# Four-layer cross-attention on one core: engine orders and PSUM seats made anew from the fifth group's first layer on

## The chip, the core and the metric

The kernel runs on one core of a Trainium2 chip. Its time is device microseconds (us) of one execution. The kernel before was run three times: 557.09, 555.94 and 558.67 us, median 557.09.

## What is computed

The input is x (64 sequences of 128 tokens, 256 features), a context of 64 x 128 x 128 and a second context ("side") of the same shape. Four layers of cross-attention follow each other, all in float32:

```
L0: x = x + softmax(Q K^T / 16) V Wo + bo         Q from x, K and V from ctx
L1: two attentions on normalised x (a: keys from normalised ctx, v: from normalised side);
    x = x + out_a + out_v;  x = x + norm(x) @ fc_W + fc_b
L2: x = norm(softmax over the queries(Q K^T / 16) V + x) * gamma + beta
L3: x = x + softmax(Q K^T / 16) V Wo + bo
```

## The kernel before

**Tiling.** Two sequences make a group; there are 32 groups, each of which passes through all layers. The weights of an attention are folded first (M = Wq Wk^T, N = Wv Wo), so that a layer costs per group: queries (Q), scores (S), a transposition of the probabilities (PT), the weighted context (O) and the projection (OUT). Operands of Q, OUT and a few other products are split into a high and a low part ("hi", "lo"), three products of 256 columns for one. Of the names used below, OUT_fc is the dense part of L1; B2 and V_L2 are the keys' and values' products of L2, made from ctx alone; S_L2 and OUT_L2 are L2's scores and output.

**Engines.** TensorE (PE) does the products, and each result stays in one of eight PSUM banks until ScalarE (ACT) or VectorE (DVE) has read it. ACT does exponentials, copies and "hi" parts, DVE does maxima, sums, "lo" parts and residuals, GpSimd (POOL) does normalisations and row additions, and SyncE (SP) issues every DMA. An attention's last steps are a chain over three engines: PE O_L3, ACT oT_hi_L3 (line 994), DVE oT_lo_L3 (line 1219), PE OUT_L3 (lines 817 to 819). PT_L3 (line 784) likewise goes over ACT's pT_L3 to O_L3 (line 806).

**Through DRAM.** The transposed x of L2 takes a way over DRAM: DVE turns blocks (turn_x3), SP stores them (send_x3, line 638), waits, and loads them back in four DMAs (fetch_x3, lines 640 to 643, issued at line 628). S_L2(g) (line 916, matmuls at line 927) waits for them. The keys of L1 go the same way (send_keys, fetch_keys). Other loads on the same SP queue are load_x (512 KB, line 610), load_ctx (line 614) and load_side (128 KB, line 618); DVE's stats_keys (line 1353) waits for load_side. The store of a group's output is at line 647.

**What sets the order.** Three tables written out by hand or by a planner: STARTS (line 26) has for each of 98 repeated steps 32 numbers, one for a group; PREPARATIONS (line 226) the same for the weights' steps; SEATS (line 243) has the PSUM bank of each use. `timetable()` (line 339) sorts all steps by their number, and each engine's program issues its own steps in that order (`steps_of`, line 545). The numbers have no other use: an engine waits for semaphores alone. COPIES (line 293) has the number of buffers of each tile. A step that takes a bank waits (`bank_for`, line 511) until the bank's last reader has raised its semaphore:

```python
for _, g, name in table:
    if g < 0 and name in preparation:
        preparation[name]()
    elif g >= 0 and name in program:
        program[name](g)
```

Each engine works through its list in order; a step whose input is late holds all that stands behind it on that engine.

Of the kernel before, what the change touches and what calls it, by code (L numbers as in the profile page):

```python
# [50 lines left out]
    "x_bias": [1697, 1869, 2066, 3305, 4131, 5182, 5811, 6496, 10163, 11795, 12108, 12768, 15404, 17497, 18858, 19907, 21118,  # L51
        22461, 24303, 25654, 28257, 29078, 31779, 32290, 33176, 34642, 37610, 38730, 42590, 42715, 43856, 44563],
    "stats_keys": [771, 2568, 3008, 3271, 4384, 4883, 5686, 6916, 7694, 8715, 10618, 13463, 14449, 15514, 16126, 18926, 21377,
        22491, 23556, 24936, 27272, 28423, 29924, 30855, 33415, 35291, 36211, 37748, 39987, 41024, 43612, 44736],
# [1647 lines left out]
```

## Time and profile before

| | |
|---|---|
| median of three runs | 557.09 us |
| span of the profiled execution | 557.1 us (equal to the median run's time) |
| PE, DVE, ACT, POOL busy | 98%, 86%, 80%, 86% of the span |
| matmul records | 4492 |
| DMA | 76.58 MB, 137 GB/s on average |

PE's busy time is the union of its records; a 256-column matmul has a record of 281 ns, and the next one begins about 0.12 us after it, so records overlap. Waits are put down to what ended last.

### The profile page before, as it was taken

Reading aid. Unit: us, or ns where it says so; the run is one execution under the profiler, and the core shown is the slowest. Engines: PE = TensorE matmul, PEld = TensorE weight load, DVE = VectorE, ACT = ScalarE, POOL = GpSimd, SP = SyncE. Lnnn points to the kernel's source line nnn. Section 1 sums busy time; section 2 is a strip of 40 time slices with the busy share of each in tenths; the row PEclk is TensorE's granted clock in tenths of the full one; section 3 lists DMA queues with packets and bytes.
Section 4 is the critical chain, followed back from the end, with each engine's and each line's share of the span. In section 5 each row is a group of like instructions: output and inputs, shape, how many; then the busy total and the mean of one; then the engine's idle time right before and its main releaser. Section 6 shows DMA issues by size and latency. Waiting matters only on the chain.

```text
span 557.1 us, 16210 instructions
## 1 busy us (share of the span) xinstructions
PE 545.8 (98%) x4492; PEld 534.9 (96%) x4492; DVE 478.4 (86%) x1472; ACT 447.2 (80%) x1568; POOL 480.7 (86%) x672
## 2 busy tenths in 40 slices
PE   8999999999999999999999999999999999999995
PEld 7999999999999999989999999999999999999994
DVE  2588799888999889989897997999898987998884
ACT  2799987889778797869879798877888979798663
POOL 4999997999988989979997899977999998766793
PEclk9999999999999999999999999999999999999999
DMA  8993472344553345453247263453433432221112
GB/s 238 352 326 126 118 215 90 121 147 149 172 168 111 113 143 152 149 174 124 80 139 202 67 190 102 145 172 122 139 122 115 124 105 78 77 96 58 39 40 95
DMA packets 74440, 76.58 MB, mean 137 GB/s; under 512 B 7664, under 2 KB 58224, under 8 KB 74352
## 3 DMA queue, kind: packets, MB, share of 16 engines
q1 hardware_dynamic: 74352, 75.55, 43.0%
q8 instruction: 38, 0.62, 0.5%
q14 instruction: 50, 0.41, 0.3%
HBM read 50.87 MB, written 24.64 MB: 136 GB/s over the span
## 4 chain that ended last, share of the span: by engine, by line
PE 87%; POOL 4%; DMA 3%; issue 2%; DVE 2%; SPq 1%; ACT 1%; DVEq 0%; POOLq 0%; ACTq 0%
PE bank L793 15%; PE bank L806 10%; PE bank L800 9%; PE bank L776 7%; PE bank L817 5%; PE bank L819 5%; PE bank L818 5%; PE bank L949 5%; PE bank L927 5%; PE bank L784 5%; PE bank L830 4%; PE bank L902 3%; PE bank L903 3%; PE bank L904 3%; DMA side_in<-in_side 1%
## 5 line engine op out<-in xcount | busy, mean ns | idle before, releaser
L1065 ACT ACTIVATE prob_L<-bank,neg_max_L 128x128 f32<-128x128 f32 x320 | 114.5, 375 | 15.7 <-DVE neg_max_L L1376 13.6
L1065 ACT ACTIVATION_READ_ACCUMULATOR prob_L<-bank,neg_max_L 128x1 f32 x320 | 68.3, 214 | 0.0
L1376 DVE TENSOR_REDUCE neg_max_L<-bank 128x2 f32<-128x256 f32 (+1 forms) x128 | 60.5, 479 | 7.1 <-PE bank L800 4.3
L1546 POOL TENSOR_TENSOR rstd_ln<-var_eps_ln,minus_half 128x2 f32<-128x2 f32 x64 | 45.2, 707 | 18.5 <-ACT var_eps_ln L1078 18.2
L994 ACT ACTIVATE oT_hi_L<-bank 128x256 fp32r<-128x256 f32 (+1 forms) x96 | 44.4, 471 | 12.4 <-PE bank L806 11.1
L1219 DVE TENSOR_TENSOR oT_lo_L<-bank,oT_hi_L 128x256 fp32r<-128x256 f32 (+1 forms) x96 | 47.2, 501 | 5.6 <-ACT oT_hi_L L994 4.9
L994 ACT ACTIVATE probT_L<-bank 128x256 f32<-128x256 f32 (+1 forms) x96 | 44.4, 470 | 9.0 <-PE bank L784 8.6
L1333 DVE BATCH_NORM_STATS2 stats_ln<-x 128x6 f32<-128x256 f32 x128 | 47.5, 413 | 0.2
L1219 DVE TENSOR_TENSOR xT_lo_L<-bank,xT_hi_L 128x512 fp32r<-128x512 f32 x64 | 43.1, 677 | 3.7 <-ACT xT_hi_L L994 3.5
L1611 POOL TENSOR_TENSOR x_bias<-x,bias_fc 128x512 f32<-128x512 f32 x32 | 41.1, 1285 | 5.8 <-DVE x L1409 5.8
L1588 POOL TENSOR_TENSOR xT_lo_L<-x_in,xT_hi_L 128x512 fp32r<-128x512 f32 x32 | 41.2, 1286 | 5.4 <-ACT xT_hi_L L994 5.4
L1597 POOL TENSOR_TENSOR x_bias<-x_in,bias_L 128x512 f32<-128x512 f32 x32 | 41.1, 1285 | 3.7 <-DVE x L1403 3.7
L994 ACT ACTIVATE xT_hi_L<-bank 128x512 fp32r<-128x512 f32 x64 | 38.7, 610 | 6.8 <-PE bank L776 4.3
L1628 POOL TENSOR_TENSOR x_res<-x_res,bias_L 128x512 f32<-128x512 f32 x32 | 41.1, 1285 | 2.5
L817 PE MATMUL bank<-N_hi_L,oT_hi_L 128*128 128x256 f32 x128 | 40.1, 314 | 2.7 <-DVE oT_lo_L L1219 2.7
L784 PE MATMUL bank<-ident,prob_L 128*128 128x128 f32 x256 | 42.6, 273 | 0.2 <-ACT prob_L L1065 0.2
L1604 POOL TENSOR_TENSOR x_bias<-x,bias_L 128x512 f32<-128x512 f32 x32 | 41.2, 1286 | 1.8 <-DVE x L1403 1.3
L1171 ACT ACTIVATE prob_L<-prob_L,inv_total_L 128x128 f32<-128x128 f32 x128 | 41.5, 418 | 1.3 <-DVE inv_total_L L1383 1.2
L1626 POOL TENSOR_TENSOR x_res<-xhat_ln,gamma_row 128x512 f32<-128x512 f32 x32 | 41.2, 1287 | 1.4 <-DVE y L1403 1.1
L793 PE MATMUL bank<-xT_hi_L,M_hi_L 128*128 128x256 f32 x128 | 40.2, 314 | 0.0
L800 PE MATMUL bank<-ctx_in,qT_L 128*128 128x128 f32 x256 | 38.5, 275 | 0.5 <-ACT qT_L L1127 0.3
L806 PE MATMUL bank<-probT_L,ctx_in 128*128 128x128 f32 x256 | 38.5, 275 | 0.0
(228 smaller groups left out, 2294.2 us busy)
## 6 DMA issues: line engine op xcount, KB each, us to landing
x_in<-in_x SPq DMA_DIRECT2D x32, 512.0 KB, 3.8
ctx_in<-in_ctx SPq DMA_DIRECT2D x32, 256.0 KB, 2.8
keys_out<-keys_turned SPq DMA_DIRECT2D x32, 256.0 KB, 2.2
keysT<-keys_out SPq DMA_DIRECT2D x128, 64.0 KB, 2.0
out<-y SPq DMA_DIRECT2D x32, 256.0 KB, 2.3
x_out<-x_turned SPq DMA_DIRECT2D x30, 256.0 KB, 2.2
x3T<-x_out SPq DMA_DIRECT2D x120, 64.0 KB, 2.3
side_in<-in_side SPq DMA_DIRECT2D x32, 128.0 KB, 2.7
```

The lines of the kernel that those rows point to most:

```text
L784: last = tr(block(bank, b), src[:, b, :], ident[:])
L793: last = mm(bank[:, i * TOK:(i + 1) * TOK], w[:, t, :], x[:, t, :], start=t == 0 and n == 0, stop=t == T - 1 and n == 2)
L800: last = mm(block(bank, b), block(at(qT[k], g), b), kT[:, b], start=True, stop=True)
L806: last = mm(block(bank, b), natural[:, b, :], block(at(probT[k], g), b), start=True, stop=True)
L817: mm(to, h, N_h[:], start=i == 0, stop=False)
L994: activation(to, of, ACT.Copy).then_inc(done[step], 1)
L1065: last = activation(at(prob[k], g)[:, b, :], block(bank, b), ACT.Exp, bias=at(neg_max[k], g)[:, b:b + 1], accum_out=at(total[k], g)[:, b:b ...
L1171: last = activation(p[:, b, :], p[:, b, :], ACT.Copy, scale=at(inv_total["L1"], g)[:, b:b + 1])
L1219: dve.tensor_tensor(to, of, hi.bitcast(F32), ALU.subtract).then_inc(done[step], 1)
L1333: last = dve.bn_stats(st[:, n, :], tile)
L1376: dve.tensor_reduce(at(neg_max[k], g)[:], scores, AX.X, ALU.max, negate=True).then_inc(done[f"max_{k}"], 1)
L1546: pool.tensor_tensor(at(rstd[k], g)[:], at(var_eps[k], g)[:], minus_half[:, 0:n], ALU.pow).then_inc(done[f"rstd_{k}"], 1)
```

## The change

STARTS, PREPARATIONS and SEATS have new numbers. Code, operations, sizes, transfers, the counts of steps and COPIES are the same. What that does to the orders, counted over both tables:

| engine | steps | same from the start | of the groups' steps: in another place | moved by at most |
|---|---|---|---|---|
| PE | 760 | 53 | 276 of 738 | 6 places |
| ACT | 821 | 63 | 430 of 802 | 19 |
| DVE | 856 | 54 | 488 of 830 | 14 |
| POOL | 465 | 49 | 190 of 448 | 4 |
| SP | 269 | 48 | 80 of 252 | 4 |

PE's first 53 steps are everything up to O_L0(3); the first other step is Q_L0(4), which now stands ahead of Q_L1(1). The first changed seat is that of O_L0(2). The places of the order that the prediction speaks of, before and after (for PE all steps from the first to the last named are shown):

```
PE before: OUT_fc:16 V_L2:18 PT_L0:21 OUT_L1:17 OUT_L0:19 O_L0:20 B2:19 T_fc:17 O_L0:21 ... OUT_fc:17 S_L2:16
PE after:  V_L2:18 OUT_fc:16 OUT_L1:17 OUT_L0:19 O_L0:20 PT_L0:21 B2:19 T_fc:17 O_L0:21 ... OUT_fc:17 S_L2:16

PE before: OUT_fc:29 T_L3:26 Q_L3:25 PT_L1:31 OUT_L1:30 O_L1:31 Q_L3:26 S_L2:28 T_fc:30 S_L3:25 S_L3:26 OUT_L1:31 OUT_fc:30 S_L2:29
PE after:  Q_L3:25 OUT_fc:29 T_L3:26 PT_L1:31 OUT_L1:30 O_L1:31 Q_L3:26 T_fc:30 S_L2:28 S_L3:25 S_L3:26 OUT_L1:31 OUT_fc:30 S_L2:29

PE before, its last steps: Q_L3:31 PT_L3:30 S_L3:31 OUT_L3:29 O_L3:30 PT_L3:31 OUT_L3:30 O_L3:31 OUT_L3:31
PE after, its last steps:  Q_L3:31 PT_L3:30 S_L3:31 OUT_L3:29 O_L3:30 PT_L3:31 O_L3:31 OUT_L3:30 OUT_L3:31

SP before: send_x3:1 load_x:10 fetch_keys:5 fetch_x3:1
SP after:  send_x3:1 load_x:10 fetch_keys:5 fetch_x3:1

SP before: send_x3:13 load_x:22 fetch_x3:13 load_side:20
SP after:  send_x3:13 fetch_x3:13 load_x:22 load_side:20

SP before: store:19 send_x3:23 fetch_keys:26 load_ctx:30 fetch_x3:23
SP after:  send_x3:23 store:19 fetch_keys:26 fetch_x3:23 load_ctx:30

SP before and after: send_x3:11 store:8 fetch_x3:11 load_side:18
DVE before: stats_lnf:12 inv_L1:13 lo_L1:14 lo_fc:12 max_L2:10 stats_keys:18 oT_lo_L0:15
DVE after:  stats_lnf:12 lo_L1:14 inv_L1:13 lo_fc:12 max_L2:10 stats_keys:18 oT_lo_L0:15
```

Four pairs of PE steps stand much closer after the change: PT_L0(21) to O_L0(21) has 10 matmul records between them (before 32), O_L0(26) to OUT_L0(26) 34 (56), O_L0(11) to OUT_L0(11) 46 (66), O_L3(6) to OUT_L3(6) 14 (26).

The diff replaces some 240 lines of the three tables by as many; seven of the 98 steps of STARTS and one of SEATS stand here:

```diff
...
-    "load_x": [598, 1078, 1126, 1894, 2374, 2725, 3569, 4395, 5587, 6765, 7583, 10302, 12074, 12282, 12907, 15654, 17636, 18997,
-        20046, 21631, 23999, 24736, 25793, 28591, 29405, 31918, 32429, 33813, 36493, 38744, 40228, 42729],
+    "load_x": [601, 1162, 1206, 2146, 2593, 2857, 3698, 4528, 5720, 6938, 7753, 10486, 12264, 12359, 13159, 15955, 18382, 19948, 20287,
+        22107, 24296, 25097, 26385, 29048, 29848, 32379, 33041, 34327, 37241, 39144, 41092, 43370],
...
-    "OUT_fc": [6138, 7159, 7982, 9037, 10990, 13848, 14797, 15736, 16958, 18486, 21833, 22342, 23604, 25187, 27472, 28252,
-        30515, 32012, 34172, 35842, 36837, 37408, 39262, 41138, 43479, 45273, 46832, 48070, 49970, 50536, 51505, 52290],
+    "OUT_fc": [6281, 7303, 8127, 9183, 11169, 14021, 15057, 15973, 17199, 18745, 22153, 22681, 23944, 25531, 27855, 28655, 31011,
+        32458, 34659, 36331, 37345, 37917, 39792, 41708, 44086, 45883, 47483, 48699, 50622, 51279, 52195, 53000],
...
-    "PT_L3": [9824, 10923, 11976, 13647, 15353, 18200, 19683, 20454, 22204, 23332, 26697, 27843, 28951, 29632, 31811, 33532,
-        34855, 37112, 39106, 40148, 41708, 43026, 44424, 46402, 47678, 51910, 51932, 53255, 53348, 53710, 54068, 54358],
+    "PT_L3": [10072, 11148, 12249, 13954, 15590, 18503, 20051, 20801, 22472, 23762, 27061, 28320, 29376, 30059, 32257, 33999, 35345,
+        37531, 39636, 40815, 42254, 43704, 44821, 47033, 48419, 52601, 52623, 53939, 54050, 54421, 54762, 54993],
...
-    "O_L3": [10120, 11154, 12163, 13803, 15535, 18353, 19882, 20610, 22527, 23488, 26807, 28093, 29088, 29909, 31968, 34357,
-        35019, 37221, 39218, 40659, 41804, 43208, 44590, 47086, 48825, 52245, 52431, 53370, 53504, 53862, 54268, 54510],
+    "O_L3": [10373, 11378, 12364, 14163, 15772, 18611, 20323, 20979, 22867, 23900, 27243, 28432, 29513, 30333, 32413, 34802, 35580,
+        37872, 39748, 40979, 42392, 43816, 45199, 47714, 49608, 52955, 53300, 54072, 54206, 54603, 54941, 55083],
...
-    "OUT_L3": [10347, 11455, 12554, 14132, 16337, 19133, 20227, 20936, 22803, 24091, 27213, 28597, 29267, 30129, 32243, 35064,
-        35322, 37732, 39448, 41279, 42128, 43408, 44839, 48212, 50289, 52476, 52861, 53549, 53907, 54197, 54439, 54682],
+    "OUT_L3": [10596, 11655, 12756, 14492, 16664, 19413, 20529, 21237, 23144, 24478, 27597, 28957, 29692, 30554, 32690, 35510, 35855,
+        38285, 39935, 41850, 42717, 44015, 45404, 48863, 50808, 53142, 53565, 54250, 54532, 54870, 55127, 55316],
...
-    "V_L2": [2417, 2675, 3265, 4136, 5334, 6750, 7735, 9409, 10808, 12092, 16135, 17144, 18972, 19997, 22226, 23217, 25738,
-        27888, 30657, 31354, 32549, 33114, 33855, 37266, 37661, 39035, 40588, 41849, 43850, 44212, 46144, 48327],
+    "V_L2": [2538, 2801, 3383, 4253, 5477, 6893, 7677, 9620, 10989, 12271, 16373, 17385, 19342, 20368, 22565, 23535, 26083, 28184,
+        30940, 31779, 32925, 33652, 34322, 37730, 38170, 39565, 41184, 42553, 44459, 44843, 46754, 49069],
...
-    "fetch_x3": [6982, 7851, 8766, 9749, 11882, 14532, 15410, 16351, 17684, 19399, 22498, 23090, 24216, 25848, 28212, 29213,
-        31726, 32921, 34802, 36541, 37672, 38478, 40036, 41974, 44210, 46265, 47556, 48794, 50583, 51216, None, None],
+    "fetch_x3": [7137, 8009, 8880, 9877, 12029, 14800, 15721, 16607, 18148, 19568, 22803, 23438, 24818, 26195, 28598, 29658, 32152,
+        33282, 35264, 36985, 38286, 38954, 40608, 42468, 44867, 46902, 48202, 49480, 51227, 51899, None, None],
...
-    "N_L1v": [5],
+    "N_L1v": [2],
```

## Rows read from the trace of the kernel before

**Rows 1.** The page's first two parts, whole span: busy us (share) and count; granted clock.
```profile
PE 545.8 (98%) x4492; PEld 534.9 (96%) x4492; DVE 478.4 (86%) x1472; ACT 447.2 (80%) x1568; POOL 480.7 (86%) x672
...
PEclk9999999999999999999999999999999999999999
```

**Rows 2.** The page's fourth part, the chain that ended last, share of span by engine.
```profile
PE 87%; POOL 4%; DMA 3%; issue 2%; DVE 2%; SPq 1%; ACT 1%; DVEq 0%; POOLq 0%; ACTq 0%
```

**Rows 3.** Windows: stretch, length, busy us (count) per engine, clock, DMA share, GB/s.
```profile
0.00:20.00 20.00, 17.45 (x85) 15.46 (x86) 6.64 (x25) 8.08 (x21) 11.73 (x30) 1.00 0.87 271
...
80.00:100.00 20.00, 19.40 (x165) 19.13 (x164) 18.35 (x57) 14.60 (x58) 16.10 (x25) 1.00 0.40 111
...
200.00:250.00 50.00, 48.95 (x416) 48.46 (x415) 44.63 (x138) 40.32 (x140) 43.38 (x61) 1.00 0.49 153
250.00:300.00 50.00, 49.34 (x419) 48.86 (x418) 44.95 (x140) 43.63 (x161) 46.20 (x62) 1.00 0.41 125
300.00:350.00 50.00, 49.72 (x416) 48.86 (x415) 44.02 (x136) 41.95 (x143) 45.74 (x64) 1.00 0.41 129
...
400.00:450.00 50.00, 49.79 (x418) 49.12 (x418) 44.93 (x139) 41.69 (x146) 47.17 (x64) 1.00 0.37 118
...
530.00:557.00 27.00, 21.25 (x160) 18.92 (x158) 17.93 (x50) 13.82 (x50) 17.27 (x24) 0.97 0.21 70
sum 557.00, PE 545.76 PEld 534.93 DVE 478.45 ACT 447.15 POOL 480.67; mean PE 36.38 PEld 35.66 DVE 31.90 ACT 29.81 POOL 32.04
```

**Rows 4.** Windows again, the last stretch alone.
```profile
552.50:557.10 4.60, 0.90 (x6) 0.69 (x6) 0.88 (x2) 0.00 (x0) 0.00 (x0) 0.80 0.34 114
```

**Rows 5.** Chain of waits around S_L2(1) and S_L2(13): start, us, what.
```profile
84.35 0.60 issue
84.94 1.13 PE bank L927 x8
...
266.55 0.66 issue
```

**Rows 6.** Timeline of SP's queue before those two: start, us, issue.
```profile
76.54 0.33 SPq L610 DMA_DIRECT2D x_in<-in_x  x1
...
78.87 1.85 SPq L628 DMA_DIRECT2D x3T<-x_out  x4
...
261.44 0.35 SPq L610 DMA_DIRECT2D x_in<-in_x  x1
261.89 1.80 SPq L628 DMA_DIRECT2D x3T<-x_out  x4
```

**Rows 7.** Chain, then timelines of DVE and PE's loads, before OUT_L0(15).
```profile
234.84 4.52 DMA side_in<-in_side
...
239.46 0.49 DVE L1333 BATCH_NORM_STATS2 stats_keys<-ctx_in 128x6 f32<-128x128 f32 x2 [1.80 <-DMA side_in<-in_side]
...
241.17 0.19 PEld L817 LDWEIGHTS bank<-N_hi_L,oT_hi_L 128*128 128x128 f32 x1 [1.25 <-DVE oT_lo_L L1219]
```

**Rows 8.** Timeline of PE at S_L2(16), then at S_L2(29).
```profile
326.38 0.28 PE L904 MATMUL bank<-F_hi,xT_lo_fc 128*128 128x256 f32 x1
326.57 1.13 PE L927 MATMUL bank<-x3T,B 128*128 128x128 f32 x8
...
522.25 0.28 PE L904 MATMUL bank<-F_hi,xT_lo_fc 128*128 128x256 f32 x1
522.37 1.05 PE L927 MATMUL bank<-x3T,B 128*128 128x128 f32 x8
```

**Rows 9.** Timeline of the last steps: DVE's and ACT's before OUT_L3(30), PE's O_L3(31) and OUT_L3(31).
```profile
549.52 0.41 DVE L1219 TENSOR_TENSOR oT_lo_L<-bank,oT_hi_L 128x256 fp32r<-128x256 f32 x1
549.64 0.38 ACT L994 ACTIVATE probT_L<-bank 128x256 f32<-128x256 f32 x1 [0.25 <-PE bank L784]
...
550.79 0.61 PE L806 MATMUL bank<-probT_L,ctx_in 128*128 128x128 f32 x4
...
552.42 0.39 PE L817 MATMUL bank<-N_hi_L,oT_hi_L 128*128 128x256 f32 x1 [1.02 <-DVE oT_lo_L L1219]
```

More of the change, by code:

```diff
@@ L45 @@
-    "load_side": [214, 1558, 1606, 1654, 4035, 4658, 5462, 6340, 7441, 8164, 10008, 13048, 13987, 14842, 15754, 17902, 20774,
[5 rows of a table removed]
[L51 to L54, printed above, removed]
@@ L211 @@
-    "fetch_keys": [3843, 4466, 4975, 5800, 7201, 7659, 8977, 11642, 13747, 14340, 15211, 16940, 19159, 21191, 22040, 23608,
[11 rows of a table removed]
-}
-PREPARATIONS = {"run_up": 164, "M_L2": 534, "k_L2": 709, "N_L0": 1000, "n_L0": 912, "M_L0": 1364, "M_L1v": 1452, "m_L0": 1541, "m_L1v":
[14 rows of a table removed]
+    "load_x": [601, 1162, 1206, 2146, 2593, 2857, 3698, 4528, 5720, 6938, 7753, 10486, 12264, 12359, 13159, 15955, 18382, 19948, 20287,
[5 rows of a table added]
+    "load_ctx": [257, 1708, 1752, 2285, 2329, 2373, 2417, 2461, 2505, 2549, 10442, 11738, 12433, 14232, 15911, 18680, 20392, 21215,
[3 rows of a table added]
@@ new lines @@
+    "hi_ctx": [813, 2514, 2654, 3319, 3559, 4360, 5652, 7112, 8200, 9728, 11277, 12403, 16506, 17575, 19482, 20823, 23074, 24781,
[5 rows of a table added]
+    "lo_ctx": [863, 2651, 2915, 3685, 5236, 5707, 7118, 7933, 9733, 11799, 12884, 16747, 18431, 20086, 20551, 23231, 24351, 26270,
+        28631, 31280, 31985, 33353, 34121, 34837, 37853, 38572, 40588, 41297, 43363, 44625, 45524, 47495],
+    "load_side": [213, 1796, 1840, 1884, 4094, 4762, 5590, 6497, 7599, 8318, 10170, 13296, 14320, 15442, 16012, 18338, 21098, 22151,
[5 rows of a table added]
@@ new lines @@
+    "x_bias": [1749, 1935, 2128, 3436, 4267, 5306, 5979, 6677, 10335, 11992, 12227, 13027, 15675, 17714, 19097, 20155, 21351, 23107,
+        24682, 26022, 28439, 29484, 32247, 32756, 33668, 35129, 38112, 39111, 43238, 43432, 44376, 45208],
+    "stats_keys": [642, 2698, 3143, 3404, 4534, 5155, 5928, 7079, 7869, 8896, 10819, 13791, 14844, 15781, 16399, 19111, 21725, 23093,
+        23907, 25290, 27649, 29168, 30359, 31290, 33908, 35773, 36749, 38296, 40531, 41597, 44107, 45464],
+    "rstd_keys": [933, 2985, 4087, 4516, 5137, 5812, 6578, 7517, 8376, 10236, 13357, 14531, 15225, 16197, 19289, 23301, 23566, 23665,
[15 rows of a table added]
@@ new lines @@
+    "stats_lnf": [6047, 6984, 7738, 8732, 10614, 13697, 14681, 15480, 16518, 18418, 21630, 22281, 23649, 24836, 27276, 28324, 31033,
+        31877, 34120, 36233, 37000, 37453, 39533, 41308, 43724, 45830, 47097, 48061, 50150, 50587, 51758, 52302],
+    "rstd_lnf": [6510, 7325, 8106, 9369, 10791, 14048, 15157, 15799, 16679, 18643, 21835, 22480, 24082, 25141, 27732, 28843, 31553,
+        32179, 34315, 36419, 37422, 37686, 39968, 41758, 44059, 46293, 47688, 48544, 50416, 51257, 52121, 52448],
+    "lo_fc": [6201, 7207, 7988, 9105, 11058, 13911, 14963, 15900, 16732, 18665, 22035, 22528, 23814, 25231, 27437, 28538, 30854,
+        31971, 34291, 36173, 37257, 37700, 39687, 41471, 43988, 45755, 47375, 48599, 50433, 51048, 51997, 52868],
@@ new lines @@
+    "store": [10799, 12219, 13034, 15486, 17086, 19992, 20730, 21625, 23393, 25052, 28832, 29438, 30346, 30882, 32936, 35739, 36184,
[3 rows of a table added]
+    "eps_keys": [844, 2897, 3589, 3608, 4665, 5773, 6184, 7380, 8338, 9806, 11772, 14445, 14983, 16046, 16620, 20119, 22604, 23406,
[3 rows of a table added]
+    "eps_lnf": [6470, 7239, 8066, 9330, 10720, 13942, 14964, 15688, 16639, 18583, 21736, 22426, 24042, 25077, 27693, 28523, 31139,
[7 rows of a table added]
+    "turn_keys": [1372, 4149, 4929, 5686, 6922, 7419, 8826, 11353, 13529, 14094, 15142, 16095, 18277, 21097, 21904, 23587, 24700, 26772,
+        28664, 30126, 31161, 33748, 35585, 36426, 37194, 38818, 41093, 43826, 45042, 46787, 47668, 49638],
@@ L247 @@
     "n_L0": [2],
-    "B2": [4, 7, 2, 5, 6, 0, 1, 3, 6, 7, 5, 5, 4, 7, 1, 3, 3, 3, 1, 7, 7, 4, 3, 4, 6, 3, 7, 7, 5, 3, 5, 4],
+    "B2": [4, 7, 2, 2, 6, 6, 2, 5, 6, 2, 2, 4, 6, 1, 6, 7, 7, 3, 2, 1, 6, 7, 3, 2, 7, 4, 5, 0, 6, 0, 2, 0],
     "M_L0": [5],
@@ L251 @@
     "m_L0": [7],
-    "Q_L0": [0, 4, 3, 0, 6, 4, 0, 1, 5, 1, 1, 6, 0, 0, 5, 6, 6, 7, 7, 6, 5, 6, 2, 2, 0, 3, 3, 0, 0, 0, 3, 6],
+    "Q_L0": [0, 4, 3, 0, 4, 3, 6, 5, 7, 6, 1, 1, 0, 2, 4, 6, 6, 2, 3, 6, 4, 7, 1, 6, 7, 4, 4, 0, 2, 1, 2, 0],
     "m_L1v": [1],
-    "S_L0": [5, 6, 5, 0, 1, 3, 1, 5, 3, 5, 5, 6, 6, 1, 0, 7, 4, 0, 3, 2, 3, 3, 1, 6, 3, 3, 3, 7, 5, 4, 4, 3],
+    "S_L0": [5, 6, 5, 0, 5, 5, 5, 2, 7, 5, 2, 4, 3, 4, 4, 2, 1, 6, 7, 1, 4, 2, 7, 1, 1, 5, 4, 4, 2, 2, 3, 0],
     "n_fc": [4],
@@ L268 @@
     "M_L1a": [0],
[1 row of a table removed]
[1 row of a table added]
     "mean_M_L1a": [4],
[1 row of a table removed]
[1 row of a table added]
     "m_L1a": [3],
[5 rows of a table removed]
-    "T_fc": [1, 5, 6, 5, 6, 6, 5, 1, 5, 6, 7, 3, 7, 4, 2, 7, 1, 5, 4, 5, 3, 3, 6, 2, 1, 3, 6, 5, 7, 7, 1, 5],
-    "OUT_fc": [1, 5, 6, 5, 5, 5, 0, 1, 5, 6, 1, 7, 7, 6, 4, 0, 2, 2, 0, 6, 2, 4, 3, 2, 1, 3, 6, 7, 3, 7, 3, 0],
[10 rows of a table removed]
[5 rows of a table added]
+    "T_fc": [2, 2, 6, 1, 3, 4, 6, 1, 4, 5, 7, 2, 2, 6, 4, 2, 7, 6, 6, 1, 1, 6, 7, 0, 7, 1, 2, 5, 2, 2, 2, 7],
+    "OUT_fc": [2, 2, 6, 1, 3, 4, 1, 1, 0, 5, 5, 7, 2, 5, 2, 0, 0, 0, 2, 1, 3, 6, 4, 7, 7, 1, 2, 4, 3, 2, 3, 4],
[9 rows of a table added]
 }
```

34 lines of the change are left out of this document (10 added, 24 removed), and 371 rows, old and new, of tables (PREPARATIONS, SEATS, STARTS).

## The prediction

> **What bounds the kernel now.** I read the busy shares first: PE is busy 98% of the span, the next engines 86%, and the granted clock is at its upper level (2.4 GHz) in every slice [rows 1]. The chain that ended last is 87% PE [rows 2]. So the time is PE's work plus the time in which PE stands still, and a change that keeps all operations can only alter the second. I then looked for that in windows [rows 3]: a stretch's length less PE's busy time is its idle time. It is 2.55 us in the first 20 us, 0.60 in 80 to 100, 1.05 in 200 to 250, 0.66 in 250 to 300, 0.28 in 300 to 350, 0.21 in 400 to 450, and 5.75 in the last 27. All together 557.00 - 545.76 = 11.24 us; what those seven leave, 0.14, is scattered. Last I read, for each of the larger ones, what PE waited for, and asked whether the new order changes that wait.
>
> **What can change at all.** The first 2.55 us lie before O_L0(3), where the order is kept. Of the last 5.75 us, 4.60 - 0.90 = 3.70 lie in the stretch that holds only the last projection, the last residual on DVE and the last store [rows 4]; these stay. There remain 2.94 us in the middle (0.60 + 1.05 + 0.66 + 0.28 + 0.21 + 0.14) and 5.75 - 3.70 = 2.05 us near the end, 4.99 us in all. If the new order lost none of it, the time would be 557.1 - 5.0 = 552.1 us. That is the most that can be had by these rows, and more than any single step promises.
>
> The sum is made against the profiled execution, whose span, 557.1 us, is also the median of the three runs (557.09), so nothing is to be added around it.
>
> The Trainium skill (Perfetto Trace Analysis, Identifying the Most-Contended Engine) warns that PE's busy share is no good measure of headroom, as pipelined instructions look smaller in the trace. The rows bear it out in part: records of 0.28 us begin 0.12 us apart [rows 8], so a delay of up to 0.16 us between two matmuls leaves no idle time. By that rule more than 5.0 us could be had; the sum here does without it.
>
> **The end of the kernel.** Before, PE issued OUT_L3(30) ahead of O_L3(31). OUT_L3(30) had to wait for DVE's oT_lo, which ended at 549.52 + 0.41 = 549.93; the copy of probabilities that O_L3(31) needs ended at 549.64 + 0.38 = 550.02 [rows 9]. O_L3(31) nevertheless began only at 550.79, since six projections stood ahead of it. After the change it comes first and can begin at about 550.07 (0.05 after its input). That is 0.72 us earlier. From O_L3(31) to OUT_L3(31) it is 552.42 - 550.79 = 1.63 us, a chain over ACT and DVE; OUT_L3(30) with its six matmuls (6 x 0.12 = 0.7) now fits into it after four records of O_L3(31) (about 0.5). DVE's residual of group 30, which stood ahead of the last oT_lo, comes later, which may give another 0.1. Ends: 0 (if the copy is delayed by as much) and 1.0 (the whole wait at OUT_L3(31)). I take -0.75 us.
>
> **S_L2(13).** PE stood 0.66 us [rows 5] because the four fetches for it, issued from 261.89 on, came right behind a 512 KB load_x issued at 261.44 [rows 6]. The new order puts load_x(22) behind the fetch; PE's steps between OUT_fc(13) and S_L2(13) are the same in number. The fetch is issued 0.45 us sooner and has the DMA engines to itself. Ends: 0.45 (issue alone) and 0.66. I take -0.6 us. S_L2(23) has the same change with a 256 KB load_ctx(30); it holds the 0.21 us of 400 to 450. I take -0.2 us. load_x(22) itself is issued some 2 us later, behind the four fetches (1.80 us [rows 6]); Q_L0(22), the first product that needs it, stands 338 matmul records after S_L2(13) (some 40 us at 0.12), which covers it.
>
> **S_L2(1).** Its 0.60 us [rows 5] have the same cause (load_x issued at 76.54, the fetch at 78.87 [rows 6]), and there the new order is the same. It stays: 0.
>
> **OUT_L0(15).** The largest single wait, 1.25 us seen by PE's loads, came over DVE: stats_keys(18) waited 1.80 us for side_in, which needed 4.52 us to land, and oT_lo_L0(15) stood behind it [rows 7]. SP's order before that load and DVE's order at that place are the same after the change. It stays, unless this load lands faster in that run: ends -1.05 and 0, I take 0. The 0.28 us of 300 to 350 I leave as well.
>
> **New waits.** V_L2(18) now stands ahead of OUT_fc(16), so OUT_fc(16), and all that goes over DRAM from it, is six matmuls (0.70 us) later, while S_L2(16) keeps its place. It had no reserve: it began 0.19 us after the matmul before it where 0.12 is usual [rows 8]. That is 0 to 0.77 us of new wait; I take 0.6. Q_L3(25) likewise moved ahead of OUT_fc(29). S_L2(29) began without a wait (0.12 us [rows 8]), so its reserve is between nothing and more than it loses; 0 to 0.7, and I take 0.3. The remaining differences (276 PE steps in another place, 488 on DVE) can't be priced one by one. Most stand with both their suppliers and users moved alike. I allow -0.2 to +3.0 for them and take +0.1, because a gain there has little to remove.
>
> **Seats.** O_L0(2) is the first with another bank. A new bank costs something only where its last reader on ACT or DVE comes later than the step's own input. None of PE's larger waits above is one for a bank. Ends: 0 and one copy (0.38 [rows 9]); I take 0.
>
> **The sum.** -0.75 - 0.6 - 0.2 + 0.6 + 0.3 + 0.1 = -0.55, so 557.1 - 0.55 = 556.5 us: 0.1% less, which a measurement of this kernel (three runs of before lie between 555.94 and 558.67) can't tell from no change. About 0.5%, 2.8 us, can be told; it is used below for faster (under 554.3) and slower (over 559.9).
>
> **Rival 1, the idle time goes.** The new order hands DMA results and DVE's results to PE in time nearly everywhere, the stats_keys wait included, and at least 2.8 of the 5.0 us go. For it: of the middle's 2.94 us, 0.60 + 0.66 + 0.21 are waits of the DMA kind and 1.05 + 0.28 come over one DVE step behind a load, few causes that a new order can avoid. Against: for two of the largest, S_L2(1) and OUT_L0(15), 1.65 us together, the order is the same. It gives 557.1 - 3.6 = 553.5 us.
>
> **Rival 2, slower: covers made too thin.** At four places a PE step has moved close to the one that needs its result. PT_L0(21) to O_L0(21) has 22 records fewer between them (2.6 us of cover at 0.12), O_L0(26) to OUT_L0(26) 22 (2.6), O_L0(11) to OUT_L0(11) 20 (2.4), O_L3(6) to OUT_L3(6) 12 (1.4). ACT and DVE take their lists in order: if the copy between the two stands behind another step there, PE waits. For it: the largest such wait now is 1.25 us [rows 7], and DVE, at 86%, has short reserves. Against: 10 records, the least that is left, are 1.2 us, and one copy takes 0.38 [rows 9]. It decides from about three such places on; with four at 1.25 us the time is 556.5 + 5.0 = 561.5 us.
>
> The Trainium skill (TensorE: Matmul & The Clock Gate, What's actually happening) has PE's clock depend on recent activity, with a throttled default. By that rule long new waits would cost more than their length. Here the granted clock stayed at the upper level with waits of up to 1.25 us, and fell to a mean of 0.80 only in the stretch after the last matmul [rows 4]. No row shows matmuls at the lower level within the loop, so this stands outside the sums.
>
> **Rival 3, the moved order brings nothing, the losses are the transfers' own.** Waits at DMA results depend on how long a transfer happens to take (1.80 us at one of 32 stats_keys); then the sum of middle waits stays near 2.9 us at other places, and only the end gains: 557.1 - 0.75 = 556.4 us. It has the same time as my sum and differs by its rows alone.
>
> **Chances.** My sum 0.38 and rival 3 0.17, together within 0.5%: 0.55. Rival 1, faster: 0.25. Rival 2, slower: 0.20. The likeliest case's own range is 554.5 to 558.7: the sum with all gains at their larger and losses at their smaller ends, 557.1 - 1.0 - 0.66 - 0.21 - 0.2 = 555.0, and another 0.5 for the wait at OUT_L0(15); above, 557.1 + 0.77 + 0.7 with no gain but the end's, and 0.9 of other waits. To leave no more than 2 in 10 outside, the range goes to 552.8 (rival 1 nearly whole) and 560.6 (rival 2 with three places).
>
> **What would show it.** In the profile after, PE's busy time is again near 545.8 us. The first 46 us are alike. OUT_L3(30) starts right behind O_L3(31), and the wait at OUT_L3(31) is about 0.4 us in place of 1.02. S_L2(13) and S_L2(23) start without a wait, S_L2(1) with 0.6, S_L2(16) with up to 0.8. The prediction is wrong if PE's idle time between 46 and 530 us is under 1 us or over 5.5, or if a new wait of over 1.3 us stands at one of rival 2's four places.

## The result, and the profile after

The changed kernel took 563.19 us (median of four runs, 562.09 to 564.32), the kernel before 556.6 on the same chip (four runs). The ratio is 1.010, interval 1.007 to 1.013: 1% slower. The prediction said no change that can be told (556.5, range 552.8 to 560.6) and gave slower 0.20. Four slow executions of the experiments below (one of e11, one of e15, two of e12), at 602.5 to 1922.3 us, are left out of every median and ratio.

The profiled execution took 563.4 us and spans 561.5; the difference, 1.9 us, is that of every run here within 0.15. First the page's busy times, granted clock and chain shares:

```profile
PE 550.6 (98%) x4492; PEld 537.1 (96%) x4492; DVE 479.1 (85%) x1472; ACT 446.0 (79%) x1568; POOL 481.3 (86%) x672
...
PEclk9899999999999999999999999999999999999998
...
PE 95%; DMA 1%; ACT 1%; SPq 1%; issue 1%; DVE 0%; DVEq 0%; ACTq 0%
```

Against [rows 1], PE's busy time has grown by 4.8 us for the same 4492 matmuls, and its idle time is 561.5 - 550.6 = 10.9 us, where it was 557.1 - 545.8 = 11.3. So the longer span shows as busy time and not as idle time. Against [rows 2] the chain has gone over from POOL, DMA and DVE to PE. The windows (stretch, length, busy us and count per engine, clock, DMA share, GB/s) say the same:

```profile
0.00:20.00 20.00, 16.32 (x70) 14.65 (x70) 5.33 (x22) 6.33 (x15) 11.08 (x30) 0.91 0.84 258
80.00:100.00 20.00, 18.75 (x154) 17.93 (x153) 17.47 (x59) 13.78 (x49) 14.73 (x24) 1.00 0.47 132
200.00:250.00 50.00, 50.00 (x424) 49.37 (x423) 44.82 (x138) 41.87 (x147) 44.90 (x63) 1.00 0.51 159
250.00:300.00 50.00, 50.00 (x417) 49.02 (x417) 45.82 (x142) 42.30 (x154) 47.15 (x64) 1.00 0.42 132
300.00:350.00 50.00, 49.96 (x419) 49.16 (x419) 43.58 (x136) 41.10 (x146) 44.96 (x64) 1.00 0.43 137
400.00:450.00 50.00, 49.90 (x417) 49.11 (x415) 43.51 (x137) 43.30 (x154) 48.03 (x66) 1.00 0.34 106
...
556.90:561.50 4.60, 0.92 (x6) 0.72 (x6) 1.56 (x4) 0.00 (x0) 0.00 (x0) 0.67 0.34 114
```

The first row belongs to a part that the change leaves alone. Split at the start of O_L0(3), ahead of which PE's order is the same, the windows of the kernel before, then of the changed one, are:

```profile
0.00:46.19 46.19, 43.65 (x286) 40.69 (x287) 27.59 (x108) 30.06 (x92) 36.96 (x62) 1.00 0.87 285
46.19:557.10 510.91, 502.12 (x4208) 494.23 (x4206) 450.86 (x1365) 417.10 (x1477) 443.71 (x611) 1.00 0.40 124
```

```profile
0.00:48.31 48.31, 44.63 (x287) 41.91 (x288) 27.13 (x108) 30.09 (x92) 37.02 (x62) 0.96 0.84 273
48.31:561.50 513.19, 505.99 (x4208) 495.23 (x4206) 451.95 (x1365) 415.87 (x1477) 444.27 (x611) 1.00 0.40 124
```

Of the 4.4 us between the two spans 2.1 lie ahead of the first changed step, so in this pair of traces about half of the difference is not the change's: the product of L0's weights starts at 14.79 us where it was 13.76, and the granted clock falls behind it (e2). In e2 below O_L0(3) starts at 46.40 us and the time is just as long, so the start does not explain the median. Behind O_L0(3) the same 4208 matmuls take 2.3 us longer, though this execution of the kernel before was itself slower than usual (see "The base").

Read beside [rows 3, 4], PE looks nearly perfect from 200 us on: 0.00, 0.00, 0.04 and 0.10 us of idle time where there were 1.05, 0.66, 0.28 and 0.21 us. One window over the whole stretch from 46 to 530 us shows what is wrong with that reading, first the kernel before:

```profile
46.00:530.00 484.00, 481.06 (x4053) 475.50 (x4052) 433.12 (x1317) 403.46 (x1428) 426.64 (x588) 1.00 0.41 127
```

And the changed kernel:

```profile
46.00:530.00 484.00, 482.31 (x4033) 474.12 (x4031) 431.80 (x1314) 401.04 (x1424) 426.40 (x584) 1.00 0.41 127
```

PE is 1.25 us busier and has done 20 matmuls fewer; at 0.12 us each that is 2.4 us lost. The repetition e1 of the kernel before did 4077 in the same 484 us, in an execution 2 us under its median, as this one was some 2 us over. The number of matmuls in a window is the honest measure here, PE's busy time is not. The busy time of its weight loads, the second figure, does fall, from 475.50 to 474.12 us.

Now the steps that the prediction named. Below are the chain of waits at S_L2(1), then the timeline of PE at S_L2(13), S_L2(16), S_L2(29) and OUT_L0(15). These rows answer to [rows 5, 7, 8]:

```profile
86.93 1.25 issue
88.18 1.13 PE bank L926 x8
```

```profile
269.99 0.28 PE L829 MATMUL bank<-ctxT_lo,M2T_hi 128*128 128x256 f32 x1
270.11 0.38 PE L926 MATMUL bank<-x3T,B 128*128 128x128 f32 x2
...
329.31 0.28 PE L903 MATMUL bank<-F_hi,xT_lo_fc 128*128 128x256 f32 x1
329.43 0.49 PE L926 MATMUL bank<-x3T,B 128*128 128x128 f32 x3
...
526.48 0.28 PE L903 MATMUL bank<-F_hi,xT_lo_fc 128*128 128x256 f32 x1
526.60 0.38 PE L926 MATMUL bank<-x3T,B 128*128 128x128 f32 x2
...
244.92 0.36 PE L816 MATMUL bank<-N_hi_L,oT_hi_L 128*128 128x256 f32 x1
```

S_L2(1) waits 1.25 us (before 0.60), the others not at all. The end, on PE's timeline, answers to [rows 9]:

```profile
553.53 0.44 PE L783 MATMUL bank<-ident,prob_L 128*128 128x128 f32 x2
554.44 0.71 PE L805 MATMUL bank<-probT_L,ctx_in 128*128 128x128 f32 x4 [0.47 <-ACT probT_L L993]
554.90 0.37 PE L816 MATMUL bank<-N_hi_L,oT_hi_L 128*128 128x256 f32 x1
...
555.58 0.28 PE L818 MATMUL bank<-N_hi_L,oT_lo_L 128*128 128x256 f32 x1
556.86 0.38 PE L816 MATMUL bank<-N_hi_L,oT_hi_L 128*128 128x256 f32 x1 [0.99 <-DVE oT_lo_L L1218]
```

OUT_L3(30) does start right behind O_L3(31), but OUT_L3(31) still waits 0.99 us.

This is what a small wait looks like. PE at OUT_fc(3) before:

```profile
91.17 1.03 PE L949 MATMUL bank<-V,prob_L 128*128 128x256 f32 x4
91.85 0.47 PE L902 MATMUL bank<-F_hi,xT_hi_fc 128*128 128x256 f32 x1
```

PE, then DVE, of the changed kernel at the same step:

```profile
94.43 1.03 PE L948 MATMUL bank<-V,prob_L 128*128 128x256 f32 x4
95.36 0.36 PE L901 MATMUL bank<-F_hi,xT_hi_fc 128*128 128x256 f32 x1
```

```profile
93.92 0.69 DVE L1375 TENSOR_REDUCE neg_max_L<-bank 128x4 f32<-128x512 f32 x1 [0.52 <-PE bank L799]
94.53 0.68 DVE L1218 TENSOR_TENSOR xT_lo_fc<-bank,xT_hi_fc 128x512 fp32r<-128x512 f32 x1
```

OUT_fc(3) begins 0.93 us after OUT_L2(1); before it was 0.68. Its last input, lo_fc(3), ended at 95.21 because max_L1(4) stood ahead of it on DVE. PE lost 0.25 us and the row carries no idle time, since OUT_L2's record, 1.03 us long, covers the gap. The spacing is 0.93 us in all four traces in which max_L1(4) stands ahead of lo_fc(3) (the changed kernel, e2, e4, e11) and 0.67 or 0.68 in the other fourteen.

To count such places in a trace, I took for each of PE's 707 steps behind O_L0(3) the recorded end of the last ACT, DVE or POOL step that it waits for. Within 0.20 us of PE's start, the input decides the start or nearly so. Before it was so at 42 steps (in e1, the same kernel, at 49), after at 106 (e2: 106). From here on these are called late steps. At 11 of the 106, and 1 of the 42, what came last was only the emptying of a PSUM bank.

A count doesn't say how late. For the time, I compared each late step's distance from PE's step before it with what the same pair of steps has where the input came early (over 0.30 us ahead; the lowest tenth, over all 18 traces). Together the late steps lose 7.3 us before and 6.3 in e1, 9.9 in the changed kernel, 11.7 in e2 and 10.7 in e4. This is an estimate from the traces; taking the lowest quarter in place of the tenth moves each figure by less than 1 us and leaves their sequence.

### The profile page after: what moved, and what is told of

It reads as the page before. It is cut to its first block, busy times and chain, and to the rows that moved or that the text cites. A ratio compares the mean times of both kernels' runs of the same rounds, so it can differ in the third digit from the quotient of the medians.

```text
span 561.5 us, 16210 instructions
## 1 busy us (share of the span) xinstructions
PE 550.6 (98%) x4492; PEld 537.1 (96%) x4492; DVE 479.1 (85%) x1472; ACT 446.0 (79%) x1568; POOL 481.3 (86%) x672
## 4 chain that ended last, share of the span: by engine, by line
PE 95%; DMA 1%; ACT 1%; SPq 1%; issue 1%; DVE 0%; DVEq 0%; ACTq 0%
PE bank L792 16%; PE bank L805 10%; PE bank L799 10%; PE bank L775 7%; PE bank L816 6%; PE bank L818 5%; PE bank L817 5%; PE bank L926 5%; PE bank L783 5%; PE bank L948 5%; PE bank L829 4%; PE bank L901 3%; PE bank L902 3%; PE bank L903 3%; PE bank L938 1%; DMA WkT_L<-in_L_WkT 1%
## 5 line engine op out<-in xcount | busy, mean ns | idle before, releaser
L1064 ACT ACTIVATION_READ_ACCUMULATOR prob_L<-bank,neg_max_L 128x1 f32 x320 | 66.8, 209 | 0.0
L1218 DVE TENSOR_TENSOR oT_lo_L<-bank,oT_hi_L 128x256 fp32r<-128x256 f32 (+1 forms) x96 | 47.7, 502 | 12.0 <-ACT oT_hi_L L993 11.3
```

The costliest lines, as they stand in the source:

```text
L1064: last = activation(at(prob[k], g)[:, b, :], block(bank, b), ACT.Exp, bias=at(neg_max[k], g)[:, b:b + 1], accum_out=at(total[k], g)[:, b:b ...
L1218: dve.tensor_tensor(to, of, hi.bitcast(F32), ALU.subtract).then_inc(done[step], 1)
```

## The experiments

"Replaying" below means this estimate: each step takes the length that the traces show for it, each transfer one of the times to landing that they show, and a step starts when its engine is free and all it waits for is there. Medians of the kernel before, run beside the experiments on four other occasions, lie between 557.3 and 557.9, and every ratio is against those of its own occasion. A ratio is estimated from all runs of both kernels and can differ from that of the two medians by some 0.1%. The experiments on orders write the three tables anew; their cuts show the order that comes of it, not the numbers. The traces are one execution each.

**e1, e2: the start.** e1 is the kernel before again.

> The kernel before, unchanged, to see what its runs look like in the first 20 us. Theory S (the loss is at the start, and is the run's luck, since the order is the same there): some of its runs show a clock under 0.996 and a PE wait at M_L0 of about 1.9 us, and their spans are about 2 us longer; ratio to before 1.000 within 0.3%. Theory O (the loss is made by the new order from group 4 on): all its runs have clock 0.998, span 554 to 557, and none shows the drop.

e2 puts matmuls into the wait ahead of the first weights' product, since in the changed kernel's trace PE waited 1.78 us there and the granted clock fell behind it. Windows of the changed kernel:

```profile
16.00:18.00 2.00, 2.00 (x12) 2.00 (x11) 0.76 (x2) 0.65 (x2) 1.62 (x3) 0.50 0.94 345
18.00:20.00 2.00, 2.00 (x14) 2.00 (x14) 1.25 (x5) 0.99 (x4) 1.92 (x4) 0.70 1.06 381
```

```diff
+FILL = 8
...
+                    if a == "L0":
+                        bank = bank_for(pe, f"M_{a}")
+                        for _ in range(FILL):
+                            mm(block(bank, 0), mean_of_D[:], mean_of_D[:], start=True, stop=True)
                     pe.wait_ge(weights[f"{a}_qk"], TWO)
...
```

> The changed kernel with eight 128-column matmuls of constants added on PE ahead of the wait for L0's weights (M_L0), whose result is overwritten. They lie in a wait of 1.9 us and last about 1.8 us. If the clock's fall after that wait is a part of the loss (theory S), clock is 0.998 again, the stretch 14 to 20 us is shorter by about 1 us, and the time is 561.5 to 562.5. If the clock's fall is not in the median run or costs nothing, the time stays 563.2 within 0.3.

e1: 557.52 (ratio 1.0004, interval 0.998 to 1.003). e2: 562.88 (1.010), mean clock 1.0 over its span. Its profiled execution took 563.03 us with O_L0(3) at 46.40 us, where e1 has 45.98. With the clock at its upper level and a start like that of the kernel before, the changed kernel is as slow, so the start is not the loss. In e1 one part of theory O missed: not all runs have a clock of 0.998 (0.989 to 1.0), and its trace has a fall of its own, at 8 to 12 us. Its runs with the lowest clocks, 0.989, 0.991 and 0.994, took 557.36, 559.34 and 555.51 us, so the clock doesn't sort them.

**e3, e4: in which part.** The tables of one kernel up to T_fc(3), about 90 us, and of the other behind it.

> The new order of all engines up to the step before T_fc(3) (about 90 us), then all remaining steps in the order of before; seats as in the changed kernel up to there, then the bank that has been free longest. Theory O with the loss between 46 and 100 us (S_L2(1) and small waits, 1.3 us in the profiles): 1.3 to 2 us over before, so 558 to 559. Theory O with the loss spread over the rest: equal to before within 0.3%. Theory S: also equal to before, or 2 us over it if the start's fall comes along.

> The reverse: the order and the seats of before up to about 90 us, then the new order with the bank that has been free longest. Theory O, loss spread over the rest: 4 us or more over before, 560.5 to 563. Theory O with the loss between 46 and 100 us, and theory S: within 0.3% of before (555 to 558).

e3: 558.83 (1.0024, 1.0007 to 1.0041). e4: 562.37 (1.0087, 1.006 to 1.011). So some 4.9 us (3.3 to 6.4) come with the new order behind 90 us, but not with it alone. From T_fc(3) on both e3 and e4 take the bank that has been free longest, which are neither the seats of before nor the change's (in e4, 586 of the 657 seats there differ from the change's). e7 below shows that such seats alone can cost 1.4 us, as much as e3 lost; how much of e4's 4.9 is theirs is open.

The traces speak for the order. e4 and the changed kernel share it, with other seats, in two executions. At 59 steps behind 92 us both start over 0.05 us later than the median of all 18 traces for their pair of steps, where before and e1 do not; together 6.6 and 6.7 us, and 53 of the 59 agree within 0.02 us. At 26 other steps it is the reverse, 5.6 us in before and 3.7 in e1. Delays that repeat like this belong to the order, not to a run or to the seats. (Where a pair is late in most traces its median hides the delay, so the two sums are not the loss.)

**e5: suppliers earlier.** Of ACT, DVE and POOL 56 steps are moved up; the first on DVE:

```diff
-stats_keys:9 max_L1:4 lo_fc:3 lo_L3:0
+stats_keys:9 lo_fc:3 max_L1:4 lo_L3:0
```

> Changed order; TensorE's own order, the seats, SyncE's queue and the first 50 us are as there. Only 56 steps of ScalarE (24), VectorE (25) and GpSimd (7), which hand TensorE its next operand or free its bank, are moved one to four places earlier in their engine's order. In the changed kernel's trace 27 TensorE steps behind 50 us found their last input later than their nominal start (6.1 us), and 37 more had under 0.1 us of reserve; before it were 15 and 10. Theory R (the loss is that suppliers stand behind another step in the order of ScalarE or VectorE, so that many small waits arise): replaying the recorded durations in this order, TensorE's waits behind 50 us go from 9.7 to 7.1 us, so the time goes from 563 to about 560.4 (559.5 to 561.5). Rival O (TensorE's own order puts its dependent steps too near each other, and the suppliers are as early as they can be): no change, 562.5 to 563.5. Rival M (the seats: a bank is emptied too late): no change either, as the seats stay.

561.23 (1.0064, 1.004 to 1.009), where the changed kernel had 1.0103 (1.007 to 1.013): about 2 us of the loss are back, PE's order and the seats being the same. The two intervals overlap a little, but six of e5's eight runs lie under the fastest of the changed kernel's four (562.09), so the direction is safe and the size is not. The median lies in theory R's range and outside both rivals'. At OUT_fc(3), PE's and DVE's timelines of e5:

```profile
91.95 1.02 PE L938 MATMUL bank<-V,prob_L 128*128 128x256 f32 x4
92.62 0.47 PE L891 MATMUL bank<-F_hi,xT_hi_fc 128*128 128x256 f32 x1
```

```profile
90.98 0.69 DVE L1208 TENSOR_TENSOR xT_lo_fc<-bank,xT_hi_fc 128x512 fp32r<-128x512 f32 x1
91.59 0.68 DVE L1365 TENSOR_REDUCE neg_max_L<-bank 128x4 f32<-128x512 f32 x1
```

The spacing is 0.67 again. There are 88 late steps in place of 106. In e5's one trace they lose 10.9 us together, between the changed kernel's 9.9 and e2's 11.7, so this figure does not show the gain.

**e6, e12: swaps in the old order.** Both swap 42 pairs of neighbours on ACT and DVE, PE's order untouched; e6 those that make PE's next input later, e12 those that don't.

```diff
 e6, DVE, the first pair
-stats_lnf:2 inv_L2:0
+inv_L2:0 stats_lnf:2
 e12, DVE, the first pair
-turn_keys:6 oT_lo_L0:5
+oT_lo_L0:5 turn_keys:6
```

> Order before the change; TensorE's, GpSimd's and SyncE's orders and the seats are as there. Only 42 pairs of neighbouring steps of ScalarE and VectorE (60 to 540 us) are swapped, each so that the step that TensorE waits for next comes one place later. Theory R: each swap makes a wait of 0.04 to 0.2 us, together 4.6 us by the recorded durations, so 557.4 becomes about 562.0 (561 to 563): the changed kernel's loss made from small swaps alone, with TensorE's order untouched. If small delays are swallowed (rival: an engine that starts late catches up, and 0.1 us per place costs nothing): 557 to 558.5.

> Order before the change, TensorE's order and seats as there; 42 pairs of neighbouring steps of ScalarE and VectorE (60 to 540 us) are swapped, as many as in e6, but only where nothing that TensorE waits for comes later. Theory R: nothing changes, 557.5 (557 to 558.2); e6's 6.5 us then belong to the lost reserve alone. Rival Z (departing from the tuned order costs by itself, so that e7 and e8 lost 1.4 and 1.6 us): 558.5 to 560.

e6: 564.09 (1.0117, 1.009 to 1.0145), 78 late steps, which lose 11.8 us. e12: 557.72 (1.0004, 0.998 to 1.003), 52, which lose 7.6. The windows of e6, then of e12:

```profile
46.00:530.00 484.00, 481.08 (x4014) 472.00 (x4013) 430.12 (x1301) 399.66 (x1415) 424.21 (x582) 1.00 0.41 127
```

```profile
46.00:530.00 484.00, 481.82 (x4051) 475.13 (x4050) 433.87 (x1317) 402.87 (x1428) 427.57 (x588) 1.00 0.41 127
```

e6 makes a loss as large as the change's (6.5 us) out of places one step too late, without touching PE's order or the seats. It is 39 matmuls behind the kernel before with the same busy time (481.08 and 481.06). The replay's 4.6 was 2 too small.

**e7: seats alone.**

```diff
...
-    "O_L0": [3, 6, 2, 3, 5, 3, 3, 7, 4, 4, 4, 0, 1, 7, 4, 4, 4, 5, 5, 5, 0, 4, 4, 4, 0, 6, 2, 5, 4, 3, 6, 6],
+    "O_L0": [3, 6, 5, 3, 2, 2, 2, 5, 7, 3, 6, 3, 7, 0, 2, 2, 5, 3, 3, 3, 4, 2, 2, 3, 6, 1, 0, 5, 1, 2, 7, 1],
...
```

From O_L0(2) on each use takes the bank that has been free longest.

> Order before the change for all engines; only the PSUM seats are dealt anew from O_L0(2) on, where the change's first new seat stands, each time the bank that has been free longest. Rival M (the new seats carry part of the loss): 558.5 to 560. Theory R: seats cost next to nothing, by the recorded durations 0.4 us: 557.4 to 558.2.

558.92 (1.0024, 1.0003 to 1.0045): 1.4 us, 0.2 to 2.5. The median lies in rival M's range, and theory R's 558.2 is inside the interval. So seats can cost about 1 us. These are other seats than the change's, whose own cost no run tells.

**e11: spread or not.**

> Order before the change to 90 us, the changed order from there to OUT_L3(13) at about 300 us, and then the order before again; seats as before up to 90 us and dealt anew behind it (the bank free longest). Against e4 (the changed order from 90 us to the end, +4.9 us) this tells whether the loss is spread. Theory R, spread: the replay gives 2.5 us of e4's 5.5, so 557.5 becomes 560.0 (559 to 561). Rival L (the loss sits in few places, the last steps above all): 557.5 to 558.5, or 562 where they lie ahead of 300 us.

559.98 (1.0034, 1.001 to 1.006), 74 late steps: with 210 of the 470 us in the new order, about two fifths of e4's loss (1.9 of 4.9 us), as a spread loss would have it. It is not proof, since e11 also has new seats from 90 us to the end.

**e8, e9, e10: mending.** A step's reserve is the time from its last input to its start. In these three, steps were moved where reserves were thinnest. e9, on PE and SP, for instance:

```diff
-PE: S_L0:4 PT_L1:0      SP: load_x:22 fetch_x3:13
+PE: PT_L1:0 S_L0:4      SP: fetch_x3:13 load_x:22
```

> Order before the change, seats as there. 11 steps of ScalarE, 12 of VectorE and 14 of TensorE are moved by one to four places where the trace of before shows TensorE with no reserve. Theory R: by the recorded durations TensorE's waits behind 50 us fall from 5.9 to 4.3 us (6.9 to 4.9 with transfers 0.3 us later), so 557.4 becomes 555.6 (555.0 to 556.6), better than both kernels. Rival (what is left of waits is the run's own jitter and moves with it): 557 to 557.8.

> Order before the change, seats as there; 17 steps of TensorE, 9 of ScalarE, 10 of VectorE and 5 of SyncE's queue are moved one to six places. Unlike e8 the places are chosen over the whole spread of times to landing that the traces so far show (fetch_x3 3.3 to 6.5 us from its first issue, load_x 3.1 to 6.6), not at one value. Theory R (reserves of TensorE's steps against the suppliers and the transfers set the time): replayed with landing times drawn from the traces, TensorE's waits fall from 6.8 to 5.5 us and its end by 2.4 us, so 557.5 becomes 555.1 (554 to 556.5). Rival Z (any departure from the order before costs 1 to 2 us through something that the replay does not hold, as in e7 and e8): 558 to 559.5.

> Changed order and its seats; 28 steps of TensorE, 23 of ScalarE, 25 of VectorE, 3 of GpSimd and 4 of SyncE's queue are moved one to six places. Theory R: replayed with landing times drawn from the traces, TensorE's waits fall from 12.9 to 8.2 us and the end by 4.1 us, so 563 becomes 559.0 (558 to 560.5), 1.5 below e5, which moved the suppliers alone. Rival (e5's gain was all there is, the rest lies in the coarse order): 561 to 562.

e8: 559.15 (1.0035, 1.0015 to 1.0054), a miss, 1.6 us slower with as few late steps (45). e9: 556.73 (0.9976, 0.9955 to 0.9997), the one order that beat the kernel before, by half of what was expected. e10: 565.60 (1.0147, 1.010 to 1.020), a clear miss: slower than the changed kernel, with fewer late steps (82). Those lose more, 12.6 us together, so the count alone ranks e10 wrongly and the time does not. Its trace has a new stall, DVE first, then PE:

```profile
256.48 0.49 DVE L1322 BATCH_NORM_STATS2 stats_keys<-ctx_in 128x6 f32<-128x128 f32 x2 [1.75 <-DMA side_in<-in_side]
...
257.68 0.66 DVE L1208 TENSOR_TENSOR xT_lo_L<-bank,xT_hi_L 128x512 fp32r<-128x512 f32 x1
```

```profile
258.48 0.36 PE L891 MATMUL bank<-F_hi,xT_hi_fc 128*128 128x256 f32 x1 [1.24 <-DVE xT_lo_L L1208]
```

It is [rows 7] at another place: a step waiting for a transfer holds back what stands behind it. That one wait does not explain all of e10; why its late steps lose so much stays open.

**e13, e14: the end.** The change's two swaps in the old order, and the same with two buffers:

```diff
...
-"oT_hi_L3": 1, "oT_lo_L3": 1
+"oT_hi_L3": 2, "oT_lo_L3": 2
...
```

> Order before the change with two swaps of the changed kernel's end: TensorE's O_L3(31) ahead of OUT_L3(30), and VectorE's oT_lo_L3(31) ahead of its residual of group 30. The prediction's step says that OUT_L3(31) then starts 0.75 us earlier after PT_L3(31) than in the kernel before (there 552.42 - 549.17 = 3.25 us). Theory B (oT_hi_L3 has one buffer, so ScalarE's copy for group 31 can't start until OUT_L3(30) has read it): from PT_L3(31) to OUT_L3(31) it stays at 3.25 to 3.35 us, as in the changed kernel (556.86 - 553.53 = 3.33), with a wait of about 1.0 us ahead of OUT_L3(31). Time 557.5 either way within 0.7.

> e13 with two buffers each for oT_hi_L3 and oT_lo_L3 in place of one. Theory B: the copy for group 31 starts right behind O_L3(31), 0.6 to 0.9 us earlier than in e13; from PT_L3(31) to OUT_L3(31) it is 2.4 to 2.7 us. If the single buffer is not the cause: 3.3 us as in e13.

e13: 557.15 (0.9993, 0.997 to 1.002), e14: 556.56 (0.998, 0.996 to 1.0003). PE and ACT of e13:

```profile
550.02 0.44 PE L773 MATMUL bank<-ident,prob_L 128*128 128x128 f32 x2 [0.20 <-ACT prob_L L1054]
...
553.35 0.39 PE L806 MATMUL bank<-N_hi_L,oT_hi_L 128*128 128x256 f32 x1 [0.99 <-DVE oT_lo_L L1208]
```

```profile
552.46 0.38 ACT L983 ACTIVATE oT_hi_L<-bank 128x256 fp32r<-128x256 f32 x1 [1.57 <-PE bank L808]
```

And of e14:

```profile
549.16 0.44 PE L773 MATMUL bank<-ident,prob_L 128*128 128x128 f32 x2 [0.20 <-ACT prob_L L1054]
...
551.72 0.39 PE L806 MATMUL bank<-N_hi_L,oT_hi_L 128*128 128x256 f32 x1 [0.23 <-DVE oT_lo_L L1208]
```

```profile
550.82 0.39 ACT L983 ACTIVATE oT_hi_L<-bank 128x256 fp32r<-128x256 f32 x1 [0.80 <-PE bank L795]
```

From PT_L3(31) to OUT_L3(31) it is 3.33 us in e13, 2.56 in e14. In e13 ACT's copy is released by the last matmul of OUT_L3(30) (line 808), in e14 by O_L3(31) (line 795). The single buffer took the gain between these two steps, 0.77 us. By their times the two kernels can't be told from the kernel before. e14 doubles oT_lo_L3 too; that it is oT_hi_L3 which held is read from ACT's releasers, and was not run apart.

**e15, e16: side_in.** Four buffers for three, in the kernel before and in e9.

```diff
...
-"side_in": 3
+"side_in": 4
...
```

> The kernel before with four buffers of side_in in place of three, orders and seats the same. VectorE's stats_keys has waited for side_in for 1.80 us in the trace of before and for 1.75 us in e10's, with TensorE's next operand behind it. load_side waits until the third group before it has been normalised, on GpSimd; with four buffers it no longer does. Theory R with the transfers' part as the replay has it: 1.1 us less, 557.5 becomes 556.4 (555.6 to 557.2). If the load's own time to landing is what counts and not when it is issued: 557.5.

> e9's order (0.24% faster than before, 556.7) with four buffers of side_in: the candidate that should beat both kernels. Theory R: another 0.5 us less than e9, 556.2 (555.2 to 557). If e15 shows nothing, this equals e9.

e15: 558.12 (1.0009, 0.999 to 1.003): nothing. e16: 556.83 (0.9997, 0.998 to 1.0015): its median is in the stated range and equals e9's, as was expected for the case that e15 shows nothing; but against the runs of before beside it there is no gain, so not even e9's is certain. e15's expectation missed.

## Why the prediction was wrong

**The step that failed** is the term for the remaining differences, which "can't be priced one by one": "I allow -0.2 to +3.0 for them and take +0.1, because a gain there has little to remove." That term is the result. The whole loss is 5.7 us by the ratio (4.0 to 7.5), e4 shows 4.9 us of loss behind 90 us (with seats of its own), and of the named steps only the end adds to it, 0.1 us. The reason given looks at gains alone. What the old order had to lose was not idle time but reserve, of which the prediction read no row. In the new order 106 of 707 PE steps have their last input within 0.20 us of their start, against 42, and such steps lose 9.9 and 11.7 us in two traces, against 7.3 and 6.3.

e6 and e12 show that this mechanism has the size, with the same number of swaps and only their places different. e5 shows that about 2 us of the change's loss are of this kind, on ACT, DVE and POOL. That the rest is of this kind too fits the traces and is argued, not shown: how the other 3 to 4 us divide between PE's own order, the seats and the transfers is open. No run has the change's seats with the old order, or the new order with the old seats, and e10, which moved PE's steps too, failed.

**Rival 2** had the right mechanism and the wrong form: four large waits, at four named places. Those places start within 0.12 us of their usual spacing. It even said that a copy may stand behind another step on ACT or DVE; it looked for that at four places only and asked for 1.25 us at each.

**What would show it** was in part blind. PE's idle time between 46 and 530 us is 484.00 - 482.31 = 1.69 us, inside the allowed 1 to 5.5, and no wait over 1.3 us stands at rival 2's places; neither of the two signs that the prediction is wrong came. Of the signs that it is right, three failed: PE's busy time was not near 545.8 us, the wait at OUT_L3(31) was 0.99 and not 0.4, and the first 46 us were not alike (O_L0(3) at 48.31 us, not 46.19), which e2's 46.40 shows to be a run's own.

The prediction's own reading, that a delay of up to 0.16 us leaves no idle time, held the answer. I used it for gains only. It works for losses as well: PE's busy time of 545.8, called constant, became 550.6 for the same 4492 matmuls. The sentence on the Trainium skill (Perfetto Trace Analysis, Identifying the Most-Contended Engine), that busy share is no measure of headroom, stands beside this reading, and the trace agrees: PE is 98% busy in both kernels, and one is 1% slower.

**The base.** To say "the profiled execution, whose span, 557.1 us, is also the median of the three runs" is to take a span for a time. With 1.9 us between the two, the profiled execution took about 559.0, some 2 us over the median; that the numbers agree is chance. e1, the same kernel, has a span of 553.7, about as much under its median. How a wait differs between two such executions shows S_L2(13). It stood 0.66 us in the base, but in e1 PE's timeline is

```profile
264.31 0.27 PE L830 MATMUL bank<-ctxT_lo,M2T_hi 128*128 128x256 f32 x1
...
264.61 0.46 PE L927 MATMUL bank<-x3T,B 128*128 128x128 f32 x2
```

so 0.18 us over the usual 0.12. Neither is the rule: in the ten traces that have load_x(22) ahead of the fetch the spacing is 0.20 to 1.68 us, median 0.80.

**S_L2(13), S_L2(23):** the mechanism was right. Issued ahead of load_x, at 265.00, the last fetch landed after 3.3 us, where it took 5.2 before and 4.6 in e1; PE did not wait. In the eight traces that have the fetch first the spacing is 0.11 to 0.22 us. Against the median of the ten others the gain is 0.7 us, so the 0.6 was about right in size. S_L2(23), priced at 0.2, had a wait of 0.37 us in two of the traces with its old place, 0.1 in one and none in the rest.

**S_L2(16), S_L2(29):** no new wait. The 0.6 and 0.3 were not paid. From the end of DVE's out_fc(16) to S_L2(16) it is 8.26 us before and 8.34 after.

**S_L2(1), OUT_L0(15):** SP's and DVE's orders are unchanged there. S_L2(1)'s wait is a run's own: 0.60 before, 1.25 after, and its spacing goes from 0.12 to 1.41 us over the traces with the old order there and from 0.34 to 1.61 over the five with the new one. OUT_L0(15), 1.25 before and 0 after, was said to stay. It did not quite: it waits in ten of the twelve traces with the old order around it and in one of the six with the new. Why is open; it is a gain, and not part of the loss.

**The end:** -0.75 predicted, about +0.1 measured: from PT_L3(31) to OUT_L3(31) 3.33 us, where it was 552.42 - 549.17 = 3.25. The prediction's chain went O_L3(31), ACT, DVE, OUT_L3(31) and left out that oT_hi_L3 has one buffer, which OUT_L3(30) must have read before ACT can write it again (e13, e14).

**Seats:** taken as 0 to 0.38. e7's other seats cost 1.4 us (0.2 to 2.5), so one copy is no safe bound for a new set of seats. In the changed kernel 11 steps, before 1, have the emptying of their bank as the last input; what that costs was not run apart.

Without the gains that did come, at S_L2(13) and OUT_L0(15), the loss would be larger still.
